# Half of a top-k mask moved off VectorE, ties folded into the comparisons, and a shorter chain for the residual weight

## The chip, the cores and the metric

One of the eight cores of a Trainium2 chip runs the program, once. The metric is the device time of one execution in microseconds. The engines are PE (TensorE: matmuls), DVE (VectorE), ACT (ScalarE), POOL (GpSimd) and SP, which only issues DMAs here. Each takes its own instructions strictly in order, and they wait for one another through semaphores.

## The reference

A layer normalisation, then an attention with 16 heads of 8 columns over 16 batches of 256 tokens, and beside it a product-key feed-forward whose 128 experts are selected per token and head:

```python
xn = _layernorm(x)                                   # x: 16 x 256 x 128
x + attention(xn) + ffn(xn)

# attention, per batch: softmax(q k^T / sqrt(8)) v for 16 heads, then @ Wo
# ffn, per token and each of 8 heads:
ts0, ti0 = top_k(s0, 4); ts1, ti1 = top_k(s1, 4)     # of 32 scores each
comb_s = ts0[..., :, None] + ts1[..., None, :]       # 16 sums
top_s, pos = top_k(comb_s, 16)                       # all 16 of them
w = softmax(top_s)
eh = gelu(down[idx] . xn)
out = sum over the 16 of up[idx] * eh * w
```

The index is `ti0 * 32 + ti1`, and a table has 128 rows, so indices beyond it are clamped to the last expert. The kernel therefore gives every expert (first key 0 to 3, second key 0 to 31) the product of two softmax weights, where both keys are among their best four, and the last expert also gets all the weight that is left.

## The kernel before

After a projection stage (until about 53 us) the program runs `NSLOT` = 128 slots, eight to a batch. A slot is a pair of heads of the attention: PE makes the scores of slot n into `SI` (L676), DVE takes their maxima (L1070), and eleven slots later (`LAG`) PE makes the scores once more into `SJ` with the maxima subtracted (L717), ACT takes the exponential (L475) and PE multiplies with the values (L737). There is one buffer `SJ`, so L717 waits for the exponential of the slot before, and the exponential waits for L717.

The feed-forward filter of one batch is cut into pieces that hang on the slot's number modulo 8, `k`, on each engine, in an order written out by hand. I call eight slots a period. In a period, for the batch before:

- POOL splits the maxima of a whole batch into two bf16 parts (`mpart`, L1320 and L1322, `split_maxima`), PE transposes them (L748), ACT copies them (`mT`, L498), and DMAs bring them to the attention operand. Only then may PE make the filter scores (L759, `scores`, k = 1) into the two banks `psH`.
- ACT copies both banks to `s_sb` (L394, k = 2), DVE finds the best eight of each of 32 rows of 32 (`MAX8`, L1096, k = 2 and 3, 16 heads-and-tiles times two key sets).
- DVE overwrites the best four of the second key set with `NEG` (`MATCH_REPLACE8`, L1109, k = 4 to 7, 16 of them, `REPLACED` cuts them over the slots), and turns that into weights: where `r_sb` equals `NEG` the exponential `z_sb`, else 0 (L1130, one `SCALAR_TENSOR_TENSOR` over 128x512, k = 0).
- POOL scales the scores (L1342 to L1345), subtracts to compare the first four keys with the best four (`order`, L1349) and with each other for ties (L1351 to L1353). ACT takes the sign (L487), squares the ties' part (L490) and turns it into "is equal" (L509). POOL adds the comparisons to a rank (L1366, L1368), adds the ties in three steps (L1374), and selects the keys of rank below 4 (L1376).
- POOL then makes the weights of the first key set (`p0`, L1383), their share (`a0`, L1393) and what is left for the last expert (L1385 to L1396), and the outer products `prod` of both token tiles (L1405, t = 0 at k = 0, t = 1 at k = 1; `FH` = 8 heads each). PE transposes these (L766, k = 3 and 4), and ACT copies them (L451).
- The attention's own output goes PE L779 (k = 5), ACT L482, DVE `rden` (L1124, k = 5, after six of the replacements), POOL `on` (L1311), PE L786, ACT `onT` (L458), PE L794 (k = 7).

Behind the slots stands a tail: the last eleven exponentials (`weights(n)`, L517, with three buffers instead of one), and the whole filter of the last batch `LB` on DVE (L1155 to L1238), while POOL finishes batch `LB - 1`. Its PE order is written out at L876 to L919.

## Time and profile before

| | |
|---|---|
| median of 3 runs | 331.07 us (329.2 to 331.9) |
| the profiled execution | 330.68 us, its span 328.9 us |
| DVE busy | 311.7 us, 95% of the span |
| PE, ACT, POOL busy | 299.7 (91%), 279.3 (85%), 265.7 (81%) us |
| mean of a period in the stage of the slots | 15.6 us |
| granted TensorE clock | 0.995 of full speed |

The span runs from the first to the last instruction; 1.8 us of the execution lie around it. In the stage of the slots all four engines are over 85% busy in every period, so the page alone doesn't say which of them sets the time; the waits within one period do.

### The profile page before, as it was taken

To read this page: it belongs to the slowest core of one execution; us is meant where nothing else is said; L and a number is where in the kernel's file an instruction comes from. 1 tells how busy PE (TensorE), PEld (TensorE's weight loads), DVE (VectorE), ACT (ScalarE), POOL (GpSimd) and SP (SyncE) were. 2 spreads that over 40 slices of the span, in tenths; PEclk is the share of its full clock that TensorE was granted. 3 is DMA by queue.
4 is the path that set the end of the run, shared out by engine and by line. 5 is a ranking of instruction groups with operands and counts; after the bars stand their busy time and mean duration, and the time that the engine had idled before them with its cause. 6 is when DMAs were issued, how large, how long until landed. Compare 5 with 4: busy or idle time off the path is not lost.

```text
span 328.9 us, 9946 instructions
## 1 busy us (share of the span) xinstructions
PE 299.7 (91%) x3181; PEld 165.7 (50%) x3181; DVE 311.7 (95%) x1387; ACT 279.3 (85%) x508; POOL 265.7 (81%) x537
## 2 busy tenths in 40 slices
PE   7999999978898999999999988988989899998796
PEld 3555554343445555555454545554555555555445
DVE  7699999889999999999999999999999999999874
ACT  3799986988888989898889888989888898989681
POOL 7389886835868898989898989898989899898940
PEclk9999999999999999999999999999999999999899
DMA  4866665417221222213130404030403120000001
GB/s 127 219 160 182 181 179 156 122 49 130 52 65 36 65 60 59 76 42 89 29 100 18 117 3 114 4 116 8 110 26 91 38 81 19 4 20 0 21 19 32
DMA packets 45889, 24.83 MB, mean 76 GB/s; under 512 B 5453, under 2 KB 45709, under 8 KB 45837
## 3 DMA queue, kind: packets, MB, share of 16 engines
q1 hardware_dynamic: 45836, 24.20, 27.4%
q8 instruction: 25, 0.41, 0.5%
q14 instruction: 28, 0.22, 0.2%
HBM read 15.54 MB, written 8.39 MB: 73 GB/s over the span
## 4 chain that ended last, share of the span: by engine, by line
DVE 66%; PE 13%; issue 13%; ACT 5%; POOL 2%; POOLq 0%; ACTq 0%
DVE negm L1070 28%; DVE top L1096 13%; DVE r_sb L1109 12%; DVE r_sb L1130 2%; PE SI L590 2%; ACT Eb L418 1%; PE SJ L843 1%; PE SJ L579 1%; ACT Eb L517 1%; DVE st L965 1%; DVE rden L1124 1%; PE SJ L582 1%; DVE Eb L953 1%; DVE fst L988 1%; DVE vhat L929 1%
## 5 line engine op out<-in xcount | busy, mean ns | idle before, releaser
L1070 DVE TENSOR_REDUCE negm<-SI 128x4 f32<-128x1024 f32 x128 | 151.8, 1197 | 1.2 <-PE SI L676 1.2
L475 ACT ACTIVATE Eb<-SJ 128x1024 f32<-128x1024 f32 x117 | 119.7, 1023 | 8.9 <-PE SJ L717 8.8
L737 PE MATMUL bank<-Eb,vhat 128*18 128x256 f32 x1024 | 68.4, 385 | 10.5 <-ACT s_sb L394 10.0
L1405 POOL TENSOR_TENSOR prod<-r_sb,a 128x1024 f32<-128x1024 f32 x28 | 53.5, 1912 | 0.0
L717 PE MATMUL SJ<-QS,KS 50*128 50x256 bf16 x484 | 47.4, 273 | 5.2 <-ACT Eb L475 4.5
L676 PE MATMUL SI<-KS,QS 48*128 48x256 bf16 x512 | 50.1, 271 | 1.1 <-DVE negm L1070 0.8
L1096 DVE MAX8 top<-s_sb 128x8 f32<-128x32 f32 x480 | 47.2, 172 | 0.9 <-ACT s_sb L394 0.9
L737 PEld LDWEIGHTS bank<-Eb,vhat 128*18 128x18 f32 x1024 | 24.2, 97 | 37.7 <-ACT s_sb L394 14.0
L1109 DVE MATCH_REPLACE8 r_sb<-top,s_sb 128x36 f32<-128x36 f32 x240 | 40.2, 176 | 0.0
L676 PEld LDWEIGHTS SI<-KS,QS 48*128 48x128 bf16 x512 | 20.3, 94 | 29.6 <-issue 22.6
L766 PE MATMUL bank<-cst,prod 128*128 128x128 f32 x240 | 33.5, 284 | 0.9 <-POOL prod L1431 0.9
L766 PEld LDWEIGHTS bank<-cst,prod 128*128 128x128 f32 x240 | 26.3, 143 | 7.3 <-issue 7.3
L717 PEld LDWEIGHTS SJ<-QS,KS 50*128 50x128 bf16 x484 | 14.3, 94 | 27.6 <-ACT Eb L475 14.0
L1268 POOL TENSOR_TENSOR Eb<-Eb,parts 128x512 f32<-128x512 f32 x16 | 18.2, 1158 | 10.9 <-ACT parts L332 8.2
L394 ACT ACTIVATE s_sb<-bank 128x512 f32<-128x512 f32 x30 | 16.4, 593 | 4.1 <-PE bank L759 4.1
L759 PE MATMUL bank<-kblk,fqT 64*128 64x128 f32 x240 | 18.5, 284 | 0.5 <-ACT s_sb L394 0.5
L1109 DVE MATCH_VALUE_LOAD r_sb<-top,s_sb 128x8 f32 x240 | 18.4, 77 | 0.0
L759 PEld LDWEIGHTS bank<-kblk,fqT 64*128 64x128 f32 x240 | 15.5, 187 | 3.6 <-ACT mT L498 2.6
L1374 POOL TENSOR_TENSOR rank<-rank,order 128x48 f32<-128x48 f32 (+2 forms) x45 | 12.7, 281 | 4.7 <-ACT order L509 0.5
L1345 POOL TENSOR_TENSOR z_sb<-s_sb,rn 128x512 f32<-128x512 f32 x15 | 15.8, 1053 | 0.0
L794 PE MATMUL bank<-wo_sb,onT 128*128 128x128 f32 x60 | 13.0, 299 | 2.5 <-ACT onT L458 0.8
L1311 POOL TENSOR_TENSOR on<-fwq_in,rden 128x256 f32<-128x256 f32 x14 | 8.8, 629 | 7.1 <-DVE rden L1124 7.1
(223 smaller groups left out, 625.5 us busy)
## 6 DMA issues: line engine op xcount, KB each, us to landing
qk_parts<-parts SPq DMA_DIRECT2D x48, 128.0 KB, 2.4
QS<-qk_parts SPq DMA_DIRECT2D x32, 96.0 KB
KS<-qk_parts SPq DMA_DIRECT2D x32, 96.0 KB
x_sb<-L_attn_x SPq DMA_DIRECT2D x8, 256.0 KB, 3.4
QS<-qk_parts SPq DMA_DIRECT2D x32, 64.0 KB
KS<-qk_parts SPq DMA_DIRECT2D x32, 64.0 KB
out<-ysb SPq DMA_DIRECT2D x16, 128.0 KB, 2.0
QS<-qk_parts SPq DMA_DIRECT2D x32, 32.0 KB
```

Source lines behind the costliest of these rows:

```text
L394: A(half(to[:, :, :, 0:NK], e).rearrange("p q u a k -> p q (u a) k"), src.rearrange("p (q g k) -> p q g k", g=4, k=NK), ACT.Copy).then_inc ...
L475: A(Eb[:, n % 4, :], SJ[:, :], ACT.Exp).then_inc(s["ex"], 1)
L676: last = mm(SI[n % 2][:, (e * BT + t) * S:(e * BT + t + 1) * S], QS[r, b % RING, pr, t * P:(t + 1) * P], KS[r, b % RING, pr, :], start=Tru ...
L717: last = mm(second(n)[:, (e * BT + t) * S:(e * BT + t + 1) * S], KS[r, b % RING, pr, t * P:(t + 1) * P], QS[r, b % RING, pr, :], start=Tru ...
L737: last = mm(psO[32 * c:32 * c + 2 * VC, (q % 2) * S:(q % 2 + 1) * S], vhat[:, v0:v0 + 2 * VC], Eb[:, (2 * g + c // 2) % 4, e0:e0 + S], sta ...
L759: last = mm(dst[e][:, q * P:(q + 1) * P], fqT[rows, r, tok:tok + P], kblk[rows, 4 * e:4 * (e + 1), :].rearrange("p g k -> p (g k)"), start ...
L766: last = mm(dst[:, t * P:(t + 1) * P], prod[:, t, h, :, :].rearrange("p i j -> p (i j)"), ident, start=(h == 0), stop=(h == FH - 1), is_tr ...
L1070: V.tensor_reduce(negm[:, bb % 2, :, :, pr].rearrange("p t e -> p e t"), SI[slot % 2][:, :].rearrange("p (e t j) -> p e t j", e=2, j=S), a ...
L1096: last = V.max(top8[:, h, a, :], s_sb[:, h, a, 0:NK])
L1109: last = V.match_replace(r_sb[:, h, :], top4[:, h, :], s_sb[:, h, 1, :], NEG)
L1268: TT(r32[:, t, :], q32[:, t, :], parts[:, c % 2, t, 0, :], ALU.subtract).then_inc(s["r_" + nm], 1)
L1405: TT(prod[:, t, :, :, :], r_sb[:, hs, 0:NK].unsqueeze(2).to_broadcast([P, FH, TOP, NK]), a0[:, hs, :].unsqueeze(3).to_broadcast([P, FH, TO ...
```

## The change

The mask: `REPLACING` puts the heads of the second token tile first in the row of replacements. DVE's L1130 now covers only the first tile (128x256). For the second tile ACT turns `r_sb` into 1 where it is `NEG` (now -2^126, so that scaled by -2^-125 and less 1 it is exactly 1) and 0 elsewhere, by a Relu at k = 6 in the place of L509, and POOL multiplies it with `z_sb` at k = 1, between the two outer products. The rows of `s_sb` and `r_sb` lose their 4 columns of padding, with which two memsets go (L1252 and L1417, the second in slot 68; the first is replaced by one of `order`).

The ties: `order` keeps them in 4 more columns beside the comparisons. Sign and Square cover 448 and 192 elements (352 and 96 before), and POOL subtracts all at once (a new 128x256 instruction, `df`) in the place of L509 and of the three additions.

The rest: the share `a0` is made first, and the weight that is left is 1 minus its sum times the second denominator, one POOL instruction less.

Besides: `rden` moves three replacements up on DVE; `psH` is turned round, so that PE's `values` at k = 2 waits for the first of the two copies only; in the tail two score groups and one `values` go ahead of `turn_products(0)`, and DVE's maxima of the last batch no longer wait for `sel`.

```diff
-                if k == 6 and 0 <= b < B:
-                    act.wait_ge(s["eq2"], b + 1)
-                    A(ties, ties, ACT.Identity, bias=one, scale=-1.0).then_inc(s["eq"], 1)
+                if k == 6 and 0 <= b < LB - 1:
+                    act.wait_ge(s["mr"], 4 * b + 2)
+                    A(r_sb[:, FH:NH, :], r_sb[:, FH:NH, :], ACT.Relu, bias=less, scale=-2.0 ** -125).then_inc(s["msk"], 1)
...
-                    A(order[:, :, :], order[:, :, :], ACT.Sign).then_inc(s["sg"], 1)
+                    A(compared, compared, ACT.Sign).then_inc(s["sg"], 1)
...
-                    V.scalar_tensor_tensor(r_sb[:, :, 0:NK], r_sb[:, :, 0:NK], NEG, z_sb[:, :, 0:NK],
+                    V.scalar_tensor_tensor(r_sb[:, 0:FH, :], r_sb[:, 0:FH, :], NEG, z_sb[:, 0:FH, 0:NK],
                                            ALU.is_equal, ALU.mult).then_inc(s["es"], 1)
...
-                    pool.wait_ge(s["sg"], b + 1)
+                    pool.wait_ge(s["eq2"], b + 1)
+                    TT(cmp[:, :, :, :], cmp[:, :, :, :], ties[:, :, :, :], ALU.subtract).then_inc(s["df"], 1)
+                    pool.wait_ge(s["df"], b + 1)
...
+                    if t == 1:
+                        pool.wait_ge(s["msk"], b + 1)
+                        pool.wait_ge(s["z1e"], b + 1)
+                        TT(r_sb[:, FH:NH, :], r_sb[:, FH:NH, :], z_sb[:, FH:NH, 0:NK], ALU.mult).then_inc(s["em"], 1)
+                        pool.wait_ge(s["em"], b + 1)
...
-        psH = [psM, psO]
+        psH = [psO, psM]
...
-                    pe.wait_ge(s["fs_ev"], 2 * (slot // 8))
+                    pe.wait_ge(s["fs_ev"], 2 * (slot // 8) - 1)
                     values(m // 2)
...
             sj(N0 + 3)
+            sj(N0 + 4)
+            values(4 * LB - 1)
+            sj(N0 + 5)
             pe.wait_ge(s["mt_ev"], B)
             pe.wait_ge(s["pr"], 4 * LB - 2)
             turn_products(0, psM)
-            sj(N0 + 4)
-            values(4 * LB - 1)
-            sj(N0 + 5)
...
-                if slot == 68:
-
-                    pool.wait_ge(s["fs"], 10)
-                    V.memset(s_last[:, :, :, NK:KP], NEG).then_inc(s["pad2"], 1)
```

POOL's queue in a period, from `on` of one batch to the first outer product, before:

```order
L1311 TENSOR_TENSOR on<-fwq_in,rden 128x256 [waits s_onp,s_ct_ev,s_rd]
L1366 TENSOR_TENSOR cm<-order 128x128 [waits s_sg]
L1374 TENSOR_TENSOR rank<-rank,order 128x16x3 [waits s_rk,s_eq]
L1374 TENSOR_TENSOR rank<-rank,order 128x16x2 [waits s_rk]
L1374 TENSOR_TENSOR rank<-rank,order 128x16 [waits s_rk]
L1322 TENSOR_TENSOR mpart<-negm,mpart 128x4x8 [waits s_mh]
L1383 TENSOR_TENSOR p<-rank,z_sb 128x64 [waits s_sel,s_ze]
L1389 TENSOR_TENSOR dinv<-dd,den 128x16 [waits s_fe]
L1405 TENSOR_TENSOR prod<-r_sb,a 128x1024 [waits s_wt,s_es,s_fa]
```

and now (here up to the second outer product; rows that are as before are left out in both):

```order
L1368 TENSOR_TENSOR order<-order 128x64x4 [waits s_eq2]
L1370 TENSOR_TENSOR cm<-order 128x128 [waits s_df]
L1322 TENSOR_TENSOR mpart<-negm,mpart 128x4x8 [waits s_mh]
L1383 TENSOR_TENSOR p<-rank,z_sb 128x64 [waits s_sel,s_ze]
L1386 TENSOR_TENSOR a<-p,dd 128x64 [waits s_fe,s_p0]
L1395 TENSOR_SCALAR p0r<-p0r 128x16 [waits s_p2]
L1409 TENSOR_TENSOR prod<-r_sb,a 128x1024 [waits s_wt,s_es,s_fa]
L1402 TENSOR_TENSOR r_sb<-r_sb,z_sb 128x256 [waits s_z1e,s_msk]
L1409 TENSOR_TENSOR prod<-r_sb,a 128x1024 [waits s_es,s_wt,s_fa,s_em]
```

Ahead of `mpart` three small instructions have become one of 128x256, and behind it another of 128x256 has come between the outer products.

PE's queue in the tail, from `sj(N0 + 3)` (into `SJ`) on, before:

```order
L717 MATMUL SJ<-QS,KS 128x256 [waits s_ex,s_mrow]
L717 MATMUL SJ<-QS,KS 128x256 x3
L766 MATMUL bank<-cst,prod 128x128 [waits s_pr,s_mt_ev]
L766 MATMUL bank<-cst,prod 128x128 x7
L717 MATMUL SI<-QS,KS 128x256 [waits s_ex]
L717 MATMUL SI<-QS,KS 128x256 x3
L737 MATMUL bank<-Eb,vhat 18x256 [waits s_ex]
L737 MATMUL bank<-Eb,vhat 18x256 x7
```

and now:

```order
L718 MATMUL SJ<-QS,KS 128x256 [waits s_ex,s_mrow]
L718 MATMUL SJ<-QS,KS 128x256 x3
L718 MATMUL SI<-QS,KS 128x256 [waits s_ex]
L718 MATMUL SI<-QS,KS 128x256 x3
L738 MATMUL bank<-Eb,vhat 18x256 [waits s_ex]
L738 MATMUL bank<-Eb,vhat 18x256 x7
L718 MATMUL SI<-QS,KS 128x256 [waits s_ex]
L718 MATMUL SI<-QS,KS 128x256 x3
L767 MATMUL bank<-cst,prod 128x128 [waits s_pr,s_mt_ev]
```

The transposes, which wait for POOL's products (`s_pr`), now stand behind two groups of scores that feed ACT.

## Rows read from the trace of the kernel before

**Rows 1.** Windows of one period each: length, then busy time of each engine
```profile
177.84:193.41 15.57, 14.38 (x177) 8.10 (x176) 15.57 (x77) 13.82 (x26) 13.98 (x32) 1.00 0.23 63
193.41:209.55 16.14, 14.31 (x177) 8.09 (x176) 15.65 (x77) 13.68 (x26) 14.23 (x33) 1.00 0.21 59
```

**Rows 2.** Lines of DVE: busy us, mean ns of one, idle before
```profile
L1109 DVE MATCH_REPLACE8 r_sb<-top,s_sb 128x36 f32<-128x36 f32 x240 | 40.2, 176 | 0.0
L1130 DVE SCALAR_TENSOR_TENSOR r_sb<-r_sb,z_sb 128x512 f32<-128x512 f32 x14 | 9.5, 676 | 0.0
...
L1222 DVE SCALAR_TENSOR_TENSOR fqT<-fqT,z_sb 128x256 f32<-128x256 f32 x2 | 0.8, 430 | 0.0
```

**Rows 3.** Timeline of POOL: start, duration in us
```profile
211.18 0.77 POOL L1383 TENSOR_TENSOR p<-rank,z_sb 128x64 f32<-128x64 f32 x1
...
221.16 0.73 POOL L1298 TENSOR_TENSOR wgT<-wgT,xnT 128x256 f32<-128x256 f32 x1
222.39 0.63 POOL L1311 TENSOR_TENSOR on<-fwq_in,rden 128x256 f32<-128x256 f32 x1 [0.50 <-DVE rden L1124]
...
224.76 0.98 POOL L1374 TENSOR_TENSOR rank<-rank,order 128x48 f32<-128x48 f32 x3
```

**Rows 4.** Lines of POOL
```profile
L1374 POOL TENSOR_TENSOR rank<-rank,order 128x32 f32<-128x32 f32 x15 | 4.5, 301 | 1.2
...
L1389 POOL TENSOR_TENSOR dinv<-dd,den 128x16 f32<-128x16 f32 x15 | 3.3, 222 | 0.0
```

**Rows 5.** Timeline of POOL around slot 68
```profile
194.52 0.20 POOL L1417 MEMSET fqT<- 128x128 f32 x1
...
194.97 0.75 POOL L1322 TENSOR_TENSOR mpart<-negm,mpart 128x32 bf16<-128x32 f32 x1
```

**Rows 6.** Timeline of DVE around slot 68
```profile
194.95 0.67 DVE L1130 SCALAR_TENSOR_TENSOR r_sb<-r_sb,z_sb 128x512 f32<-128x512 f32 x1
...
198.37 0.75 DVE L1096 MAX8 top<-s_sb 128x8 f32<-128x32 f32 x7 [0.48 <-ACT s_sb L394]
```

**Rows 7.** Timeline of PE over one period and a little more
```profile
221.13 0.39 PE L717 MATMUL SJ<-QS,KS 50*128 50x256 bf16 x4 [0.25 <-ACT Eb L475]
...
226.85 0.29 PE L748 MATMUL bank<-cst,mpart 128*32 128x128 bf16 x2
...
229.95 1.06 PE L737 MATMUL bank<-Eb,vhat 128*18 128x256 f32 x16 [0.74 <-ACT s_sb L394]
230.96 0.39 PE L717 MATMUL SJ<-QS,KS 50*128 50x256 bf16 x4
```

**Rows 8.** Timeline of ACT in the same period
```profile
220.05 1.02 ACT L475 ACTIVATE Eb<-SJ 128x1024 f32<-128x1024 f32 x1
...
221.26 0.50 ACT L487 ACTIVATE order<-order 128x352 f32<-128x352 f32 x1
221.65 1.02 ACT L475 ACTIVATE Eb<-SJ 128x1024 f32<-128x1024 f32 x1
...
229.78 1.03 ACT L475 ACTIVATE Eb<-SJ 128x1024 f32<-128x1024 f32 x1
```

**Rows 9.** Lines of ACT
```profile
L487 ACT ACTIVATE order<-order 128x352 f32<-128x352 f32 x15 | 7.5, 501 | 0.9 <-POOL order L1353 0.9
...
L490 ACT ACTIVATE order<-order 128x96 f32<-128x96 f32 x15 | 4.4, 290 | 0.0
```

**Rows 10.** Timeline of PE in the tail
```profile
309.24 1.87 PE L766 MATMUL bank<-cst,prod 128*128 128x128 f32 x8 [0.91 <-POOL prod L1431]
```

**Rows 11.** Timeline of ACT in the tail
```profile
311.69 1.02 ACT L517 ACTIVATE Eb<-SI 128x1024 f32<-128x1024 f32 x1 [2.29 <-PE SI L717]
```

**Rows 12.** Timeline of DVE in the tail
```profile
305.14 3.08 DVE L1163 MAX8 top<-fqT 128x8 f32<-128x32 f32 x32 [0.99 <-POOL rank L1376]
...
314.86 0.42 DVE L1135 TENSOR_TENSOR wgT<-bank,xnT 128x256 f32<-128x256 f32 x1 [1.45 <-PE bank L766]
...
318.18 0.36 DVE L1141 RECIPROCAL rden<-bank 128x32 f32<-128x32 f32 x1 [0.65 <-PE bank L779]
```

More of the change, by code:

```diff
@@ L28 @@
 P = 128
-NEG = -1.0e20
+NEG = -2.0 ** 126
 C_ID, C_AVG, C_GRP = 0, 128, 256
@@ L65, in program @@
     TOP = 4
-    KP = NK + TOP
     E = down.shape[0]
@@ L116, in program @@
         nm = ve
-        eps = sb("eps", [P, 2]); one = eps[:, 1:2]
+        eps = sb("eps", [P, 2]); less = eps[:, 1:2]
         vhat = sb("vhat", [P, VC + NT * VT])
@@ L182, in program @@
         HEADS = [4 * q + 2 * e + u for e in range(2) for q in range(NH // 4) for u in range(2)]
+        REPLACING = [h for h in HEADS if h >= FH] + [h for h in HEADS if h < FH]
         def half(a, e):
@@ L486, in _ @@
                     act.wait_ge(s["tie"], b + 1)
-                    A(order[:, :, :], order[:, :, :], ACT.Sign).then_inc(s["sg"], 1)
+                    A(compared, compared, ACT.Sign).then_inc(s["sg"], 1)
                 if k == 6 and 0 <= b < B:
                     act.wait_ge(s["sg"], b + 1)
-                    A(ties, ties, ACT.Square).then_inc(s["eq2"], 1)
+                    A(tied, tied, ACT.Square).then_inc(s["eq2"], 1)
                 if k == 0 and m >= -1:
@@ L926, in _ @@
             V.memset(onT[:, 0:P // 2], 0.0).then_inc(s["zeros"], 1)
-            V.memset(one, 1.0)
+            V.memset(less, -1.0)
             V.memset(eps[:, 0:1], LN_EPS).then_inc(s["eps"], 1)
@@ L1059, in inverse_squares, with inverse_heads @@
                 V.reciprocal(rn_t[:, i * P:(i + 1) * P], rn_t[:, i * P:(i + 1) * P]).then_inc(s["n2r"], 1)
+            def inverse_heads(b):
+                dve.wait_ge(s["ct_ev"], b + 1)
+                if b >= 1:
+                    dve.wait_ge(s["on"], b)
+                V.reciprocal(rden[:, :].rearrange("p (c u) -> p c u", u=2), heads[:, :, :, DH]).then_inc(s["rd"], 1)
             for slot in range(NSLOT):
@@ L1105, in _ @@
                     for i in range(REPLACED[quarter], REPLACED[quarter + 1]):
-                        if quarter == 1 and i == FH:
-                            dve.wait_ge(s["t4"], 2 * b + 2)
-                        h = HEADS[i]
+                        if quarter == 1 and i == FH - 1 and b >= 1:
+                            inverse_heads(b - 1)
+                        h = REPLACING[i]
                         last = V.match_replace(r_sb[:, h, :], top4[:, h, :], s_sb[:, h, 1, :], NEG)
@@ L1117, in _ @@
                     V.reciprocal(dd[:, :], both).then_inc(s["fe"], 1)
-                b = (slot - LAG - 10) // 8
-                if k == 5 and 0 <= b < B:
-                    dve.wait_ge(s["ct_ev"], b + 1)
-                    if b >= 1:
-                        dve.wait_ge(s["on"], b)
-                    V.reciprocal(rden[:, :].rearrange("p (c u) -> p c u", u=2), heads[:, :, :, DH]).then_inc(s["rd"], 1)
                 b = slot // 8 - 2
@@ L1156, in _ @@
                                    ALU.is_equal, ALU.mult).then_inc(s["es"], 1)
-            dve.wait_ge(s["sel"], LB)
+            dve.wait_ge(s["tie"], LB)
             dve.wait_ge(s["t4"], 2 * LB)
@@ L1175, in _ @@
             dve.wait_ge(s["p0"], LB)
+            dve.wait_ge(s["sel"], LB)
             dve.wait_ge(s["t8"], 2 * B)
@@ L1211, in _ @@
             V.reciprocal(dd[:, :], both).then_inc(s["fe"], 1)
-            dve.wait_ge(s["tie"], LB + 2)
-            for i, (lo, n, at) in enumerate(((1, 3, 0), (2, 2, 3), (3, 1, 5))):
-                dve.wait_ge(s["rk"], 4 * LB + i + 1)
-                V.tensor_tensor(rank[:, 0, :, lo:TOP], rank[:, 0, :, lo:TOP], ties[:, :, at:at + n], ALU.add).then_inc(s["rk"], 1)
-            dve.wait_ge(s["rk"], 4 * LB + 4)
+            dve.wait_ge(s["rk"], B)
             V.tensor_scalar(rank[:, 1, :, :], rank[:, 0, :, :], float(TOP), None, ALU.is_lt).then_inc(s["sel"], 1)
@@ L1251, in _ @@
             V.memset(v_tiles(0, VSPLIT)[:, :, DH:VC], 1.0).then_inc(s["vone"], 1)
-            V.memset(s_sb[:, :, :, NK:KP], NEG)
+            V.memset(order[:, :, :, :], 1.0)
             V.memset(top4[:, :, TOP:8], NEG).then_inc(s["pad"], 1)
@@ L1370, in _ @@
                         split_maxima(LB)
-                    pool.wait_ge(s["eq"], b + 1)
-                    for i, (lo, n, at) in enumerate(((1, 3, 0), (2, 2, 3), (3, 1, 5))):
-                        pool.wait_ge(s["rk"], 4 * b + i + 1)
-                        TT(rank[:, 0, :, lo:TOP], rank[:, 0, :, lo:TOP], ties[:, :, at:at + n], ALU.add).then_inc(s["rk"], 1)
-                    pool.wait_ge(s["rk"], 4 * b + 4)
-                    V.tensor_scalar(rank[:, 1, :, :], rank[:, 0, :, :], float(TOP), None, ALU.is_lt).then_inc(s["sel"], 1)
+                    pool.wait_ge(s["rk"], b + 1)
+                    V.tensor_scalar(rank[:, 1, :, :], rank[:, 0, :, :], 0.0, None, ALU.is_lt).then_inc(s["sel"], 1)
                 if k == 7 and slot // 8 < LB:
```

55 lines of the change are left out of this document (29 added, 26 removed), and 2 rows, old and new, of the table names.

## The prediction

> **What bounds the kernel now.** I read three views. The windows, cut at one period each, come first: DVE is busy for all 15.57 us of a normal period, and one period took 16.14 [rows 1]. A queue with no idle time sets the pace. But PE has 14.38 us in the same window and POOL 13.98 [rows 1], so a gain on DVE is only worth what the second slowest allows. The second view, the timelines of the other engines, is for that question: a queue that doesn't wait for DVE anywhere has the same length as DVE's by itself.
>
> *POOL* waits once in a period for DVE: 0.50 us ahead of `on`, for `rden` [rows 3]. The rest of its idle time is the gap between links of its own chains, 1.2 us over 15, so 0.08 each [rows 4]. Its own length is 15.57 - 0.50 = 15.07 us.
>
> *PE and ACT* pass the one buffer `SJ` to and fro, and the third view is their timelines in the same period. PE waits 0.25 us for an exponential and 0.74 us for ACT's copy of the filter scores [rows 7]: both are waits inside the pair. The place where the pair could wait for POOL is L748, and there the wait before its first matmul is at most some 0.04 us: I see no row with a wait on POOL or on DVE. So the pair has a cycle of its own of about 15.5 us. Three loops of 15.57, 15.07 and some 15.53 us turn side by side.
>
> **The change part by part, one period.** *DVE.* L1130 shrinks from 512 to 256 columns: 676 ns before; L1222 is the same operation at 256 and takes 430 [rows 2]: -0.246. The replacements read 32 instead of 36 columns; the nearest rate is that of the two rows just used, 246 ns for 256 columns, 0.96 ns each, so 16 x 4 x 0.96 = -0.06. DVE's loop: 15.57 - 0.31 = 15.26 us. `rden` costs the same, three replacements earlier.
>
> *POOL.* Out: the three additions, 0.98 us and a gap [rows 3, 4], -1.06; and the wait for `rden`, which comes three replacements earlier, by 0.5 us, about what the wait was. Within the rest chain one instruction of 0.22 us goes [rows 4], but the five that stay behind `p0` now each wait for the one before, where some pairs ran gapless: with 0.08 for each new gap and 0.12 of overlap that is lost I take +0.15. In: two instructions of 128x256, `df` and the mask's product. Their price isn't in the trace; the nearest rows are 0.63 and 0.73 us for the same number of elements [rows 3], and each has a link behind it, 0.08: 1.42 to 1.62, I take 1.56, nearer to 0.73, since neither reads a broadcast operand and L1298 doesn't either. The sum: 15.07 - 1.06 + 0.15 + 1.56 = 15.72.
>
> From this comes off what L1130 does to POOL. L1383 took 0.77 us [rows 3], and in the disturbed period it was L1322, of 32 elements, that took 0.75 [rows 5], each time right behind the start of L1130, which at 194.95 lasts until 195.62 [rows 6]. A POOL instruction that meets L1130 stands still until it has ended. The shorter L1130 holds it up 0.25 us less. POOL's loop: 15.47 us; bounds 15.33 (both new ones at 0.63) and 15.7 (nothing comes off).
>
> The rule behind this is in the Trainium skill, SBUF — State Buffer, section "Who interferes with whom": a DVE instruction with two SBUF inputs and a GpSimd instruction that reads SBUF exclude each other for a whole instruction, whichever began first. The rows show only the one direction, GpSimd held up; the other is a rival below.
>
> *PE and ACT.* ACT's Sign grows from 352 to 448 elements, Square from 96 to 192; with 501 and 290 ns [rows 9] an element costs 211 / 256 = 0.82 ns, so +0.08 each. Relu over 256 comes out as 290 + 160 x 0.82 = 421 ns by the same rows (bounds 0.42 and 0.55, a bias operand) in the place of L509. Square and Relu lie ahead of `onT`, for which ACT waits anyway, and cost nothing there; without that cover they would cost 0.1 to 0.2. Sign isn't covered: the exponential at 221.65 starts when Sign lets it, 1.60 after the one at 220.05 [rows 8], so +0.08 is on the pair's path. Against this, `values` at k = 2 waits for one copy instead of two. Its 0.74 us shrink by about the half, but the next scores then wait for the exponential: that ends at 229.78 + 1.03 = 230.81, handing over takes 0.06 (220.05 + 1.02 against 221.13), so 230.87 instead of 230.96 [rows 7, 8]: -0.09. With `on` and `mpart` ready earlier some 0.03 at each of L786 and L748: -0.06. The pair: 15.57 - 0.07 = 15.50 us. Bounds: 15.65 (nothing gained, Sign and Relu both on the path) and 15.35 (the whole 0.3 of the copy comes through).
>
> So DVE wins 0.31 us and the period 0.07, as PE and ACT become the bound with POOL 0.03 behind. There are 14 such periods (L1130 x14 [rows 2]): **-1.0 us**.
>
> *The period with the memset.* Slot 68's memset, 0.20 us [rows 5], pushed L1322 into the start of L1130 (194.97 behind 194.95 [rows 5, 6]), `mpart` came 0.5 us late, and through L748, `mT`, L759 and the copy DVE stood for 0.48 [rows 6]; the period lost 0.57 [rows 1]. The memset goes: **-0.57 us**, bounds 0 (L1322 meets L1130 another time) and 0.57.
>
> *The tail.* PE waits 0.91 us for POOL's product and then takes 1.87 us for eight transposes [rows 10], with the scores for ACT queued behind; ACT stands 2.29 us [rows 11]. Now two groups of scores go ahead, and ACT runs on. But the last outputs hang on DVE too, so what counts is DVE's chain of the last batch. Its waits: 0.99 for `sel`, 1.45 for PE L766, 0.65 for PE L779 [rows 12]. The first is replaced by the wait for `s_last`, copied only around the same moment: I take 0.1 from it. The second goes whole if POOL's products are made as early as before: the transposes then follow each other on PE at about 311.0 and 312.4, before DVE comes by at 313.4 (314.86 - 1.45). Of the third I take half, 0.3, and 0.1 from narrower replacements. **-2.0 us**, bounds -0.2 (another wait of DVE takes over) and -2.9.
>
> Sum against the profiled execution's 330.68 us: 330.68 - 1.0 - 0.57 - 2.0 = 327.1. This execution lies 0.4 below the median of 331.07, well inside the three runs' spread; I keep 327.1.
>
> **The rivals.** (1) *DVE's gain comes through whole.* If the pair's waits are the shadow of DVE's pace and not a loop of their own, the period falls to POOL's lower bound or DVE's 15.26. For it: DVE is the only one without idle time. Against: no row of PE or ACT shows slack towards the others, and POOL sums to 15.47. 14 x 0.31 = 4.3: 330.68 - 4.3 - 0.57 - 2.0 = 323.8.
>
> (2) *The tail gives nothing back.* DVE's chain from 305.14 on has its waits, but each can be followed by the next: ACT's exponential of `z_sb`, POOL's `p0` and `a0`. 330.68 - 1.0 - 0.57 - 0.2 = 328.9.
>
> (3) *POOL becomes the bound.* Both new instructions at their upper price and nothing off for the shorter L1130: 15.7, so +0.13 x 14 = +1.8: 330.68 + 1.8 - 0.57 - 2.0 = 329.9.
>
> (4) *Slower: L1322 meets L1130 in every period.* POOL's work ahead of `mpart` and behind it changes by more than half a microsecond each, so its phase against DVE moves. If L1322 starts within L1130, `mpart` is late and DVE stands as in rows 6, and the next period starts from the same phase. The price of one is 0.57 [rows 1], with L1130 shorter by 0.25 about 0.3 to 0.57, and 14 of these from the period before: +4.2 to +8, with the tail's gain 330.68 + 8 - 2 = 336.7 at the worst, 333 to 337. It decides once POOL's own period exceeds some 15.6, so that L1322 falls back behind the start of L1130. For it: it did happen, from 0.2 us of added work. Against: POOL gains 0.5 us by `rden` and L1322 now has less ahead of it.
>
> The skill's rule named above adds a thing to this rival: DVE too would stand, behind a GpSimd instruction that has begun. Where L1130 meets POOL's chain of 0.2 to 0.3 us instructions, that would cost DVE up to 0.3 us in a period, and DVE has about as much to spare now; no row here shows it in the stage of the slots.
>
> **How the numbers follow.** My forecast has 0.47 (325.8 to 328.4 as its own range), (1) 0.17, (2) 0.18, (3) 0.10, (4) 0.08. The time is that of the likeliest, 327.1. The range from 323.6 to 330.2 takes in (1), (2) and (3) and leaves out (4) and the ends. About 1% can be told from no change here, that is 3.3 us of 331.07: below 327.8 lie (1) and about three quarters of the forecast, together 0.52; above 334.4 most of (4), 0.07; the rest, 0.41, is the same.
>
> **What would show it.** In the profile of after: L1130 at about 430 ns; DVE with idle time in a period, 0.2 us, ahead of the maxima of SI or of the first MAX8; a period of 15.50 and none of 16.1; POOL's two new instructions between 0.63 and 0.73, and its wait for `rden` gone; PE's wait for the copy near 0.3; the Sign near 0.58; in the tail no wait of ACT above 1 us, and DVE's 1.45 gone. Wrong would be: a period of 15.3 with DVE full (rival 1), L1322 at 0.5 or more in many periods (rival 4), POOL without any wait and a period above 15.6 (rival 3), or DVE's waits in the tail that add up to 3 us as before (rival 2).

## The result, and the profile after

| | before | after |
|---|---|---|
| median | 331.5 us (329.2 to 334.3, 13 runs) | 328.85 us (327.4 to 331.2, 13 runs) |
| ratio, 95% interval | | 0.9934 (0.9908 to 0.9961) |
| profiled execution, span | 330.68, 328.9 us | 328.70, 326.9 us |
| DVE, PE, ACT, POOL busy | 311.7, 299.7, 279.3, 265.7 us | 309.0, 298.9, 280.4, 265.5 us |

The change saves 0.7%, 2.2 us (1.3 to 3.0), where 4.0 were forecast; a second measurement of the changed kernel (e11) gave 0.9921 (0.9892 to 0.9949), 2.6 us. I cut both profiled executions at the first and the last start of L1130, of which there are 14 in each, with 13 periods between them:

| us | before | after | difference |
|---|---|---|---|
| start to the first L1130 | 85.97 | 87.33 | +1.36 |
| from there to the last L1130 (13 periods) | 202.98 | 202.06 | -0.92 |
| from the last L1130 to the end | 39.95 | 37.52 | -2.43 |

The middle row is the steady work. Before, it was twelve periods of 15.57 and one of 16.13; now it is 15.23, 15.44 and eleven of 15.58. So nearly all of it comes from the one long period (-0.56) and from the first two (-0.46); the normal period, from which 1.0 us was to come, has not become shorter at all. These are the windows of two such periods, with the columns of [rows 1]:

```profile
195.96:211.54 15.58, 14.37 (x178) 8.08 (x180) 15.46 (x77) 13.90 (x26) 14.14 (x31) 1.00 0.23 61
211.54:227.12 15.58, 14.37 (x178) 8.08 (x180) 15.46 (x77) 13.90 (x26) 14.13 (x31) 1.00 0.22 63
```

DVE, the third busy time, is no longer busy throughout: it stands some 0.2 us ahead of its first MAX8 (L1104), where 0.2 was forecast, and 0.05 ahead of `rden`. The chain of the work that ended last, which before was 66% DVE, now names PE and ACT:

```profile
PE 59%; ACT 19%; DVE 12%; issue 6%; POOL 4%; POOLq 0%; ACTq 0%; DVEq 0%
```

The other views of after answer to the groups ahead of the prediction. DVE's lines, for [rows 2]:

```profile
L1116 DVE MATCH_REPLACE8 r_sb<-top,s_sb 128x32 f32<-128x32 f32 x240 | 39.7, 177 | 0.0
L1130 DVE SCALAR_TENSOR_TENSOR r_sb<-r_sb,z_sb 128x256 f32<-128x256 f32 x14 | 6.8, 484 | 0.0
```

The lines of POOL and ACT that are new or larger, for [rows 4] and [rows 9]: `df`, the mask's product, Sign, Square and Relu.

```profile
L1368 POOL TENSOR_TENSOR order<-order 128x256 f32<-128x256 f32 x15 | 10.9, 727 | 1.0 <-ACT order L492 1.0
L1402 POOL TENSOR_TENSOR r_sb<-r_sb,z_sb 128x256 f32<-128x256 f32 x14 | 10.3, 733 | 0.0
...
L489 ACT ACTIVATE order<-order 128x448 f32<-128x448 f32 x15 | 8.7, 582 | 0.7 <-POOL order L1355 0.7
L492 ACT ACTIVATE order<-order 128x192 f32<-128x192 f32 x15 | 5.5, 370 | 0.0
L511 ACT ACTIVATE r_sb<-r_sb,eps 128x256 f32<-128x256 f32 x14 | 7.2, 514 | 0.0
```

The timeline of POOL in the period from 211.5, for [rows 3]: start, duration, and in brackets the idle time before and its releaser. The wait for `rden` at `on` (L1311) is small now and no longer named; the one that is named is 0.20 us for DVE's maxima.

```profile
211.46 0.24 POOL L1389 TENSOR_TENSOR p0s<-a 128x32 f32<-128x32 f32 x1
211.77 0.28 POOL L1391 TENSOR_TENSOR p0r<-p0s 128x16 f32<-128x16 f32 x1
...
218.65 0.30 POOL L1344 TENSOR_TENSOR z_sb<-s_sb,rn 128x64 f32<-128x64 f32 x1 [0.20 <-DVE top L1104]
...
221.50 0.72 POOL L1298 TENSOR_TENSOR wgT<-wgT,xnT 128x256 f32<-128x256 f32 x1
222.34 0.63 POOL L1311 TENSOR_TENSOR on<-fwq_in,rden 128x256 f32<-128x256 f32 x1
```

But it isn't gone altogether. DVE's `rden` ends at 222.26, and `on` starts 0.08 behind it:

```profile
221.91 0.35 DVE L1067 RECIPROCAL rden<-fwq_in 128x32 f32<-128x32 f32 x1
```

L1298 ends at 222.22, and where `on` has nothing to wait for it starts 0.04 before the recorded end of the one before (as in every second period of e10). So 0.16 us of waiting are left here and 0.24 at L1344 (its 0.20 and the same 0.04), and POOL's own length is 15.58 - 0.40, about 15.2 us.

The timelines of PE and of ACT in the same period, for [rows 7] and [rows 8]:

```profile
214.38 1.06 PE L738 MATMUL bank<-Eb,vhat 128*18 128x256 f32 x16 [0.26 <-ACT s_sb L396]
215.88 0.40 PE L718 MATMUL SJ<-QS,KS 50*128 50x256 bf16 x4 [0.44 <-ACT Eb L477]
```

```profile
214.71 1.03 ACT L477 ACTIVATE Eb<-SJ 128x1024 f32<-128x1024 f32 x1
...
220.55 1.02 ACT L477 ACTIVATE Eb<-SJ 128x1024 f32<-128x1024 f32 x1
221.47 0.41 ACT L484 ACTIVATE fwq_in<-bank 128x288 f32<-128x288 f32 x1
221.76 0.58 ACT L489 ACTIVATE order<-order 128x448 f32<-128x448 f32 x1
222.22 1.02 ACT L477 ACTIVATE Eb<-SJ 128x1024 f32<-128x1024 f32 x1
```

Two things are to be seen. PE's wait for the copy shrank from 0.74 to 0.26 us, but the next scores now wait 0.44 us for the exponential: and the scores start 1.17 us behind the exponential's start (214.71 to 215.88), as before (1.18, from 229.78 to 230.96 in [rows 7, 8]). Nothing was won there, where 0.09 was counted on. And the two exponentials around the Sign start 1.67 us apart (220.55 to 222.22), 1.60 before [rows 8]: the Sign's growth lies on the path in full.

The tail, for [rows 12]. DVE's waits were 0.99, 1.45 and 0.65 us; now the second is gone:

```profile
305.71 3.07 DVE L1163 MAX8 top<-fqT 128x8 f32<-128x32 f32 x32 [1.08 <-ACT fqT L396]
...
313.26 0.42 DVE L1135 TENSOR_TENSOR wgT<-bank,xnT 128x256 f32<-128x256 f32 x1
...
316.15 0.36 DVE L1141 RECIPROCAL rden<-bank 128x32 f32<-128x32 f32 x1 [0.21 <-PE bank L780]
```

Last, the granted TensorE clock, which the prediction had left out. First two windows in the tail of the kernel before, with the busy times of PE, PE's weight loads, DVE, ACT and POOL, then the granted clock:

```profile
305.00:310.00 5.00, 3.28 (x40) 1.56 (x33) 4.56 (x50) 4.08 (x9) 4.62 (x11) 0.93 0.11 31
310.00:315.00 5.00, 5.00 (x46) 2.63 (x44) 3.55 (x23) 2.47 (x4) 3.19 (x3) 0.73 0.09 26
```

And two windows in the projection stage of the kernel after, where the kernel before has 1.00 in both:

```profile
5.00:10.00 5.00, 3.80 (x18) 2.46 (x18) 2.54 (x19) 2.95 (x10) 1.83 (x4) 0.80 0.60 159
10.00:15.00 5.00, 5.00 (x14) 2.22 (x13) 3.22 (x9) 2.94 (x8) 0.79 (x1) 0.86 0.99 268
```

Part of the time the clock stood at its lower level, 1.2 GHz. In the tail before, it fell right behind PE's wait of 0.91 us, and the eight transposes that followed took 1.87 us [rows 10] instead of the 1.09 that a second group of eight takes in the same tail. In the kernel after, the fall comes near the start (between 7.5 and 12 us), and the whole delay of 1.43 us arises there: the first maxima of the slots begin at 54.5 instead of 53.05 us, and that is the +1.36 of the first table. So the two profiled executions each hold a stretch of low clock, at different places.

### The profile page after: what moved, and what is told of

The parts are those of the page before. It is cut to its first block, busy times and chain, and to the rows that moved or that the text cites. A ratio compares the mean times of both kernels' runs of the same rounds, so it can differ in the third digit from the quotient of the medians.

```text
span 326.9 us, 9939 instructions
## 1 busy us (share of the span) xinstructions
PE 298.9 (91%) x3181; PEld 165.6 (51%) x3181; DVE 309.0 (95%) x1385; ACT 280.4 (86%) x507; POOL 265.5 (81%) x505
## 4 chain that ended last, share of the span: by engine, by line
PE 59%; ACT 19%; DVE 12%; issue 6%; POOL 4%; POOLq 0%; ACTq 0%; DVEq 0%
PE bank L738 12%; PE SJ L718 10%; ACT Eb L477 9%; PE bank L767 8%; PE SI L677 6%; PE bank L760 4%; PE bank L795 3%; ACT s_sb L396 3%; ACT onT L460 2%; PE bank L796 2%; PE bank L787 2%; PE SI L591 2%; ACT Eb L420 1%; ACT Eb L519 1%; PE SJ L844 1%
## 5 line engine op out<-in xcount | busy, mean ns | idle before, releaser
L1104 DVE MAX8 top<-s_sb 128x8 f32<-128x32 f32 x480 | 47.5, 177 | 1.9 <-ACT s_sb L396 0.5
L1116 DVE MATCH_REPLACE8 r_sb<-top,s_sb 128x32 f32<-128x32 f32 x240 | 39.7, 177 | 0.0
L767 PE MATMUL bank<-cst,prod 128*128 128x128 f32 x240 | 32.8, 280 | 0.0
L718 PEld LDWEIGHTS SJ<-QS,KS 50*128 50x128 bf16 x484 | 14.3, 94 | 35.6 <-ACT Eb L477 15.2
L1116 DVE MATCH_VALUE_LOAD r_sb<-top,s_sb 128x8 f32 x240 | 19.2, 80 | 0.0
L760 PEld LDWEIGHTS bank<-kblk,fqT 64*128 64x128 f32 x240 | 15.5, 187 | 3.6 <-ACT mT L500 2.6
L1344 POOL TENSOR_TENSOR z_sb<-s_sb,rn 128x64 f32<-128x64 f32 x15 | 4.6, 305 | 12.3 <-DVE top L1104 12.3
L358 ACT ACTIVATE Eb<-x_sb,ve,rs 128x128 f32<-128x128 f32 x32 | 13.1, 479 | 1.7 <-DVE ve L979 1.7
```

What stands on the lines that cost most here:

```text
L718: last = mm(second(n)[:, (e * BT + t) * S:(e * BT + t + 1) * S], KS[r, b % RING, pr, t * P:(t + 1) * P], QS[r, b % RING, pr, :], start=Tru ...
L760: last = mm(dst[e][:, q * P:(q + 1) * P], fqT[rows, r, tok:tok + P], kblk[rows, 4 * e:4 * (e + 1), :].rearrange("p g k -> p (g k)"), start ...
L767: last = mm(dst[:, t * P:(t + 1) * P], prod[:, t, h, :, :].rearrange("p i j -> p (i j)"), ident, start=(h == 0), stop=(h == FH - 1), is_tr ...
L1104: last = V.max(top8[:, h, a, :], s_sb[:, h, a, 0:NK])
L1116: last = V.match_replace(r_sb[:, h, :], top4[:, h, :], s_sb[:, h, 1, :], NEG)
```

## The experiments

Each is a kernel of its own, compared with the kernel before on the same chip.

**Is it PE and ACT that hold the period now?** e1 changes nothing but the place of ACT's second copy of the filter scores, from before the exponential of slot k = 2 to behind it:

```diff
-                    for e in range(2):
-                        filter_scores(s_sb, e, psH[e])
+                    filter_scores(s_sb, 0, psH[0])
...
                     A(Eb[:, n % 4, :], SJ[:, :], ACT.Exp).then_inc(s["ex"], 1)
+                if k == 2 and 1 <= b < B:
+                    filter_scores(s_sb, 1, psH[1])
```

> The changed kernel with one edit on ACT: at k = 2 the second of the two copies of the filter scores (L396) stands behind the exponential instead of ahead of it. ACT, PE, DVE and POOL do the same work. Theory A (the loop of PE and ACT over the one buffer SJ is what holds the period at 15.58 us in the changed kernel, DVE and POOL have 0.20 us to spare): the exponential at k = 2 starts 0.48 us earlier, the period falls to the next bound, some 15.38 us, 14 x 0.2 = 2.8 us less in all. Theory B (DVE's queue, 15.46 us busy, or a loop through all engines holds it): nothing or below 0.5 us. Theory C (the scores at k = 3 wait for the DMA of mT, which the table of waits names 15 times): these scores stay 3.41 us behind the end of the copy of mT, and the period stays 15.58.

Measured: 325.96 us (324.9 to 326.8, 4 runs), ratio 0.9854 (0.9823 to 0.9884); the period is 15.38 to 15.40, and the tail 37.20. No engine has less to do; one wait moved. PE's timeline shows that the wait of 0.44 us for the exponential is gone:

```profile
212.03 1.06 PE L739 MATMUL bank<-Eb,vhat 128*18 128x256 f32 x16 [0.26 <-ACT s_sb L396]
213.03 0.40 PE L719 MATMUL SJ<-QS,KS 50*128 50x256 bf16 x4
```

So the pair held the changed kernel's period at 15.58. Theory C falls as well: these scores now start 2.92 us behind the end of the copy of `mT` (209.74 + 0.37 in ACT's timeline), not 3.41.

**Did it need DVE's part of the change?** e8 gives the kernel before this same rearrangement of PE and ACT, and leaves DVE's 512 columns:

```diff
-        psH = [psM, psO]
+        psH = [psO, psM]
...
-                    pe.wait_ge(s["fs_ev"], 2 * (slot // 8))
+                    pe.wait_ge(s["fs_ev"], 2 * (slot // 8) - 1)
...
                    A(Eb[:, n % 4, :], SJ[:, :], ACT.Exp).then_inc(s["ex"], 1)
+                if k == 2 and 1 <= b < B:
+                    filter_scores(s_sb, 1, psH[1])
```

> The kernel before with PE's and ACT's part of e1 alone: psH turned round, values waits for one copy, and the second copy of the filter scores goes behind the exponential. DVE's L1130 still covers 512 columns. Theory A (three loops side by side: the pair's falls from 15.50 to some 15.31, but DVE's own 15.57 stays): period 15.57 as before, 330.9 to 331.4 us, ratio 1.000 (0.998 to 1.001). Theory B (the pair's loop is what e1 shortened and DVE only shadows it): 14 periods of -0.18, 328.7 us, ratio 0.992.

Measured: 331.3 us (10 runs), ratio 1.0019 (0.9986 to 1.0053); twelve periods between 15.56 and 15.59 and one of 16.13. Theory A: without the relief of DVE it is worth nothing. And e2 gives the kernel before the relief of DVE alone (the mask of the second token tile is left out, nothing takes its place):

```diff
-                    V.scalar_tensor_tensor(r_sb[:, :, 0:NK], r_sb[:, :, 0:NK], NEG, z_sb[:, :, 0:NK],
+                    V.scalar_tensor_tensor(r_sb[:, 0:FH, 0:NK], r_sb[:, 0:FH, 0:NK], NEG, z_sb[:, 0:FH, 0:NK],
```

> The kernel before with L1130 over 128x256 instead of 128x512, and nothing in its place (the mask of the second token tile is left out, so the output is not the reference's). Theory A: PE and ACT had a loop of 15.57 us of their own already, so DVE's 0.25 us come to nothing: period 15.55 to 15.57, DVE gets 0.2 us idle, time as before within 0.3% (the period with slot 68's memset may lose its 0.57 us). Theory B: DVE held the period: 15.32, that is 14 x 0.25 = 3.5 us less, 1.1%.

Measured: 329.57 us (10 runs), ratio 0.9947 (0.9919 to 0.9975). The period is 15.50 us, between the two theories and much nearer to A (the first one is 15.30, the one with the memset 15.88). DVE and POOL both wait in it (DVE 0.1 to 0.2 us for the copy of the filter scores, POOL 0.59 for `rden`), so what is left is the pair: 15.50 is its own length in the kernel before, 0.07 below DVE's, and all that a relief of DVE alone could bring in a normal period. From the first to the last L1130 e2 takes 201.67 us, less than the changed kernel's 202.06: there the relief is the same, and the Sign's growth stands against it. In a window of the length of [rows 1] DVE is no longer busy throughout, and PE's and ACT's work is as it was; POOL's 13.98 us are 13.76, since it stands less behind the shorter L1130:

```profile
177.84:193.41 15.57, 14.36 (x184) 8.16 (x180) 15.46 (x77) 13.78 (x26) 13.76 (x32) 1.00 0.24 62
```

(The window is cut 0.07 longer than the period.)

**What does the longer Sign cost?** e5 is the changed kernel, e6 is e1, each with a Sign over 64 of the 448 elements, so that most of the signs are left out:

```diff
-                    A(compared, compared, ACT.Sign).then_inc(s["sg"], 1)
+                    A(compared[:, :, 0:1], compared[:, :, 0:1], ACT.Sign).then_inc(s["sg"], 1)
```

> The changed kernel with ACT's Sign cut from 448 to 64 elements, so most signs of the comparisons are left out; nothing else is touched. Theory A (PE and ACT set the changed kernel's period of 15.58 us, and the longer Sign stands on their path: the interval between the exponentials around it rose from 1.60 to 1.67 us): that interval falls to some 1.50, the period to 15.42 (DVE and POOL, whose own lengths are 15.38, then bind), 13 periods of -0.16 make -2.1 us: 326.6 to 326.9, ratio to the kernel before 0.986 to 0.988. Theory B (the pair only follows DVE or POOL, or the DMA of mT): the period stays 15.58 and the time 328.9, ratio 0.993.

Measured: 326.73 us (4 runs), ratio 0.9899 (0.9847 to 0.9952), period 15.43 to 15.44, the exponentials around the Sign 1.51 apart (221.67 to 223.18 below). Theory A, to 0.02 us a period. Its profiled execution (328.97) starts its first maxima at 56.1 us, as e8 does (last section), and has a stretch of low clock behind the projection stage; the other three runs lie at 326.6 to 326.8.

```profile
221.67 1.02 ACT L477 ACTIVATE Eb<-SJ 128x1024 f32<-128x1024 f32 x1
222.59 0.41 ACT L484 ACTIVATE fwq_in<-bank 128x288 f32<-128x288 f32 x1
222.88 0.32 ACT L489 ACTIVATE order<-order 128x64 f32<-128x64 f32 x1
223.18 1.02 ACT L477 ACTIVATE Eb<-SJ 128x1024 f32<-128x1024 f32 x1
```

> As e1_after_split (the second copy of the filter scores behind the exponential), with ACT's Sign cut to 64 elements as in e5. Theory A (in e1 the pair was no longer the bound and DVE and POOL, 15.38 each by themselves, set its period of 15.39): nothing more is gained, period 15.38 to 15.40, 325.9 to 326.2 us, ratio 0.985. Theory B (the pair was still the bound in e1): the period falls by the Sign's share to about 15.25, 14 x 0.14 = 2.0 us less: 324.0 us, ratio 0.979.

Measured: 324.14 us (323.6 to 325.5, 4 runs), ratio 0.9811 (0.9766 to 0.9857), period 15.30 to 15.33. This lies between the two theories, and both had a number wrong. In this trace DVE waits nowhere in a period, so 15.32 is its own length and the bound. The 15.38 that I had read for it still held a wait: in e1 DVE stands 0.06 us ahead of its first MAX8. POOL still waits 0.14 us for DVE here (0.09 at `on`, 0.05 at L1345), so its own length is about 15.2, as in the changed kernel. The Sign still cost 0.08 in e1: there ACT waits 0.20 us for POOL's tie differences ahead of it, and then it stands in front of an exponential.

**Where does the tail's gain come from?** e3 gives the kernel before the new order of PE's tail alone:

```diff
             sj(N0 + 3)
+            sj(N0 + 4)
+            values(4 * LB - 1)
+            sj(N0 + 5)
             pe.wait_ge(s["mt_ev"], B)
             pe.wait_ge(s["pr"], 4 * LB - 2)
             turn_products(0, psM)
-            sj(N0 + 4)
-            values(4 * LB - 1)
-            sj(N0 + 5)
```

> The kernel before with PE's order in the tail of the changed one alone: two score groups and one values ahead of the transposes of POOL's products. If this order is the tail's gain: from the last L1130 to the end 37.6 us instead of 39.95 (37.51 in the changed kernel), 2.3 us in all, 0.7%. If the gain came from DVE no longer waiting for sel or from POOL's earlier products: below 0.5 us.

Measured: 330.28 us (10 runs), ratio 0.9969 (0.9951 to 0.9987), tail 38.31 us. e7 is the counterpart, the changed kernel with the same lines turned back:

```diff
+            pe.wait_ge(s["mt_ev"], B)
+            pe.wait_ge(s["pr"], 4 * LB - 2)
+            turn_products(0, psM)
             sj(N0 + 4)
             values(4 * LB - 1)
             sj(N0 + 5)
-            pe.wait_ge(s["mt_ev"], B)
-            pe.wait_ge(s["pr"], 4 * LB - 2)
-            turn_products(0, psM)
```

> The changed kernel with PE's old order in the tail: the transposes of the first outer products stand again ahead of two groups of scores. Theory A (the tail got shorter through this order, as the prediction had it: ACT's 2.29 us and DVE's 1.45 us of waiting went with it): both waits come back, the tail from the last L1130 on grows from 37.5 to about 39 us, 330.3 to 330.8 us, ratio 0.998. Theory B (the order is worth little at the full clock, as e3 and e4 have it, 38.33 and 38.39; the tail's real gain of 0.9 us is that of POOL's earlier products and the shorter DVE chain): the tail is at most 37.8 us where the granted clock stays at 1.0, the time 328.9 to 329.3, ratio 0.993 to 0.995. If the granted clock falls in the tail again, PE stands some 0.8 us or more for POOL's product just ahead of it, and the tail is up to 1.5 us longer.

Measured: 329.44 us (328.3 to 331.2, 10 runs), ratio 0.9973 (0.9946 to 1.0001), tail 37.57 us against 37.52. Theory B: in the changed kernel the order is worth 0.05 us, and its old form shows why. PE comes to the transposes, and the product is there; it doesn't wait:

```profile
308.79 1.09 PE L767 MATMUL bank<-cst,prod 128*128 128x128 f32 x8
```

**The memset of slot 68.** e4 is the kernel before with that memset two slots earlier, out of the way of L1322:

```diff
-                if slot == 68:
+                if slot == 66:
```

> The kernel before with POOL's memset of s_last issued in slot 66 instead of slot 68, behind the outer products instead of ahead of the split of the maxima. Expected if the memset pushed L1322 into the start of L1130: no period of 16.14 us, all 15.57, 0.57 us less in the profile (too little for the times). If the long period had another cause: it stays, there or elsewhere.

Measured: 329.91 us (6 runs), ratio 0.9988 (0.9952 to 1.0024). All periods are 15.57, the one of 16.13 is gone. This trace has also the kernel before with a clock of 1.00 in the whole tail, and this tail is 38.39 us, not 39.95. PE waits as in [rows 10], but the transposes take 1.06 us and not 1.87:

```profile
308.72 1.06 PE L766 MATMUL bank<-cst,prod 128*128 128x128 f32 x8 [0.89 <-POOL prod L1431]
```

In ACT's and DVE's timelines of that tail the waits of 2.29 and 1.45 us are 1.25 and 0.45. So 1.56 us of the kernel before's tail was the low clock, not the wait. The tail's gain at the full clock is 38.39 - 37.52 = 0.87 us, and by e7 PE's order has at most 0.05 of it. What has changed is POOL: its first product of the tail ends 20.16 us behind the last L1130 in e4 and 19.16 in after.

**How much of that is `rden`?** e9 is the changed kernel with DVE's reciprocal back behind three more replacements:

```diff
-                        if quarter == 1 and i == FH - 1 and b >= 1:
-                            inverse_heads(b - 1)
...
                     last.then_inc(s["mr"], 1)
+                    if quarter == 1 and b >= 1:
+                        inverse_heads(b - 1)
```

> The changed kernel with DVE's reciprocal rden moved back behind three more replacements, where it stood before. Theory A (the earlier rden is what makes POOL fast enough for the rest of the change, in the slots and in the tail, where POOL's products come 1.0 us earlier after the last L1130 than in e4): POOL waits about 0.45 us for rden again, has only 0.20 us to spare in a period, and the period grows from 15.58 to some 15.8; the tail from 37.5 to about 38.0; together +3 to +3.8 us, 332 us, ratio 1.00 to 1.005. Theory B (the wait stands beside the pair's own loop and costs nothing there, as in the kernel before): period 15.58, only the tail grows by 0.5, 329.4 us, ratio 0.995.

Measured: 330.26 us (10 runs), ratio 0.9971 (0.9944 to 0.9998), tail 37.84, and periods that alternate, after one of 15.89, between 15.58 and 15.72 (from first to last L1130 203.04 us against 202.06). Neither theory: the wait of POOL is back, 0.35 us in one period and 0.23 in the next, and costs 0.07 us a period, 1.0 in all, and 0.3 in the tail.

```profile
223.54 0.63 POOL L1311 TENSOR_TENSOR on<-fwq_in,rden 128x256 f32<-128x256 f32 x1 [0.35 <-DVE rden L1067]
```

So one reciprocal three replacements earlier, which costs nothing, carries 1.3 us of the result: without it the slots would be no faster than before. How it carries them isn't separated: in e9 POOL also meets L1130 with another instruction (L1386, 0.47 us instead of 0.30).

**Is e1 the better kernel?** e10 is e1 again, e11 the changed kernel itself, on one chip.

> The kernel of e1 once more, in more rounds and beside the changed kernel on the same chip (e11). If e1's gain is real: period 15.39 to 15.40, 325.5 to 326.3 us, 0.8 to 0.9% below the changed kernel, ratio to the kernel before 0.982 to 0.987. If it was owed to the clock of its profiled run: within 0.3% of the changed kernel.

> The changed kernel itself, unaltered, for the direct comparison with e10 and for a second trace of it: 328.6 to 329.1 us, ratio 0.992 to 0.995, period 15.58. If the granted clock stays at 1.0 in its prologue and its tail, the first maxima start at 53.0 instead of 54.5 us and the time is 327.2 to 327.5; its tail, which has no wait of PE for POOL's product, stays at 37.5.

Measured: e10 327.62 us (326.0 to 328.1, 6 runs), ratio 0.9873 (0.9837 to 0.9909); e11 328.92 us (327.4 to 329.8, 8 runs), ratio 0.9921. e11 came as expected. e10 missed both of its theories: its period is not 15.39, and its time is 0.4% under that of e11, half of what e1 had shown. e1's kernel is the better one both times, by 0.8% (0.9854 against 0.9934) and by 0.5% (0.9873 against 0.9921, on one chip, where the two intervals overlap); in the traces its 13 periods are 2.1 and 1.1 us shorter.

The difference between e1 and e10 can be read: the periods of e10 alternate between 15.42 and 15.51, since POOL meets L1131 otherwise. Here POOL and DVE in e10:

```profile
211.29 0.41 DVE L1131 SCALAR_TENSOR_TENSOR r_sb<-r_sb,z_sb 128x256 f32<-128x256 f32 x1
```

```profile
211.31 0.49 POOL L1390 TENSOR_TENSOR p0s<-a 128x32 f32<-128x32 f32 x1
```

POOL's instruction of 32 elements takes 0.49 us, or up to 0.53, in all these periods, where it takes 0.24 in e1, and L1131 takes 0.41 instead of 0.49. POOL has no wait left in every second of these periods, so this is its own loop: about 15.2 and the stall, together 15.42, above DVE's 15.32.

The changed kernel does the same in e11, and there it costs nothing. POOL's and DVE's rows of e11:

```profile
211.70 0.52 POOL L1389 TENSOR_TENSOR p0s<-a 128x32 f32<-128x32 f32 x1
```

```profile
211.72 0.41 DVE L1130 SCALAR_TENSOR_TENSOR r_sb<-r_sb,z_sb 128x256 f32<-128x256 f32 x1
```

POOL's wait of 0.20 us at L1344 has become its stall here, and the period is 15.58 as in after, since the pair sets it. So one kernel runs in two ways, with its starts shifted by some 0.02 us: POOL's instruction begins 0.03 us before L1130 in every normal period of after, e1 and e7, and DVE stands; it begins between 0.02 before and 0.01 behind it in e10 and e11, and POOL stands. What puts an execution into one or the other is not shown. It isn't the low clock from 75 to 80 us alone: e10 has it and e11 has not, and e6 has it and runs like e1. In e11 the clock is low from 7 to 11 us (0.73 and 0.93 in the two windows shown for after), its first maxima start at 54.7 us, and its period and tail are those of after, 15.58 and 37.53.

## Why the prediction was wrong, and where it was right

**The period (-0.07 x 14 = -1.0): the step that failed.** The bound was named rightly: DVE was relieved and PE and ACT set the pace; DVE idles, and rival 1 fell. The terms that failed are the two gains that were set against the Sign's +0.08, -0.09 for the copy and -0.06 at L786 and L748: neither came. The pair's own length before is 15.50 (e2), the Sign adds 0.08 as worked out (1.60 to 1.67), and 15.50 + 0.08 is the 15.58 that was measured, with nothing left for a gain. The Relu took 0.51 us and not 0.42, which leaves no mark in this sum. The slack of 0.07 under DVE is what the Sign ate. A second error hid half of the first: the pair's own cycle was read as "about 15.5" and "some 15.53", and then the terms were added to DVE's 15.57. From 15.50 they would have given 15.43. So the forecast of 15.50 is nearer to the measured 15.58 than its reasoning was, by luck. The sum also took 14 such periods; there are 13, and one of them is the memset's. Why the copy was worth nothing: the prediction counted a handover of 0.06 us from the exponential to the scores, as at the other slots, but at this place the scores start 1.17 us after the exponential's start, in both kernels, 0.14 behind its end. With 0.14 for the handover the exponential would not have let them start before 230.95 in the kernel before either, and they started at 230.96. What I gave to `on` (-0.03 at L786) is there only in the sense of e9: it prevents a loss of 0.07.

**The first two periods (-0.46).** No step had them: 15.23 and 15.44. In e2 the first is shorter too, 15.30. The likely reason is that POOL and ACT don't have a whole batch's work yet; no run tests it. They make up for nearly half of the 1.0 us that the normal periods didn't bring.

**The memset (-0.57): right,** -0.56 in the change, and e4 has it alone (16.13 to 15.57), with the mechanism of [rows 5, 6].

**The tail (-2.0): the size came out in the profile, for a wrong reason.** The profiled executions differ by 2.43 us, of which 1.56 are the clock in [rows 10 to 12]. The prediction took the durations of a stretch of lower clock (1.87 us for eight transposes) for durations of the kernel, and the 1.45 and 2.29 us of waiting that followed from them for waits that an order removes. At full clock 0.45 of DVE's 1.45 us is left, and this goes because POOL's products come 1.0 us earlier; 0.44 of the third wait went as well (0.3 was taken), and these two make the 0.87 us. The first wait, from which 0.1 was taken, grew from 0.99 to 1.08. The second was credited to PE's order, with POOL's products as early as before. They came earlier, and the order had next to no part in it (e7).

But the order isn't worthless in the kernel before: e3 gained 0.3%, about 1.0 us, with a tail that is at full clock only 0.08 us shorter. Its runs show where this may come from: the mean granted clock was at least 0.999 in 5 of 10 runs of e3 and in 4 of the 59 runs of the kernel before that stood beside the three groups of experiments. So without PE's wait the clock seems to have fallen less often, a gain in how often and not in how long, which no sum of durations holds. The changed kernel, which doesn't have the wait either, reached 0.999 in only 3 of 13 runs, so this is not settled.

**POOL (15.47, bounds 15.33 and 15.7).** Both new instructions cost the upper price, 0.73 us and a link of 0.08. Its own length is nevertheless about 15.2, under the lower bound. The largest part is the stall at L1130: in the kernel before L1383 stood 0.45 us (0.77 instead of 0.32), in after L1391 stands 0.06, so 0.39 went and not 0.25. Where POOL stands longer (e11) it is 15.42. Rival 3 fell by this.

**DVE (15.26).** It is 15.32 (e6, where DVE has no idle time). The narrower replacements saved next to nothing (176 to 177 ns each, against 0.96 ns a column that I took from another operation: 0.06 of the sum), and L1130 takes 484 ns and not 430. The latter is the second half of the rule that the prediction weighed: in after, L1130 starts at 211.49 right behind POOL's L1389, which had begun at 211.46, and stands 0.08 us; POOL's L1391 in its turn takes 0.28 us instead of 0.22. That rule is in the Trainium skill, SBUF — State Buffer, section "Who interferes with whom": of two such instructions the one that issues first keeps the other out for its whole length. The traces agree that either can stand for the other: 0.49 us for L1130 where POOL was 0.03 us ahead (after), 0.41 where it was not, and then 0.49 to 0.53 for POOL's 0.24 (e10, e11). Two details they don't bear out. In e11 POOL stands although its start is recorded 0.01 to 0.02 us before L1130's, so recorded starts this close don't tell which issued first. And the stall is shorter than the other's recorded length: L1130 stands 0.08 us, where L1389 is recorded for 0.21 us more.

**Rival 4** (a POOL instruction meets L1130 in every period) came with L1389 in place of L1322, so `mpart` was never late. In after the overlap costs 0.08 us on DVE and 0.06 on POOL; in e11, the same kernel, 0.28 at L1389 in POOL's queue in every period. Neither costs the changed kernel any time, as both queues have more than that to spare below the pair's 15.58. In e10, where the pair is faster, it costs 0.07 us a period on average (200.91 us for 13 periods against e1's 199.96).

**The time.** The steady parts give -0.92 in the loop, -0.87 in the tail and -0.07 in the stretch from the first maxima to the first L1130 (32.92 to 32.85 us): -1.86, within the interval of 1.3 to 3.0. The forecast of 327.1 lay 1.75 us under the median. That the median is in its range owes something to luck: more than half of this gain is the memset and the first two periods, and the normal period, the purpose of the change, gave nothing.

**What stays open.** Why e7 measured 0.4% more than the changed kernel (the intervals overlap) although loop and tail agree to 0.05 us: four of its ten runs lie at a span of 329.2 to 329.4 with a clock of 0.99, and three of the 13 of after at 329.3 to 329.4 with 0.98 to 0.99; none of these was profiled. And why the clock falls near the start in four traces of the changed kernel's family (after, e7, e9, e11) and not in e1, e5, e6 or e10, which have the same code there. In these four PE's first ten matmuls (L617, from 0.97 us on) had taken 3.8 to 4.2 us together, in all others 4.45. And what decides which of POOL and DVE stands at L1130.

## What to carry to other kernels

Where three loops turn side by side, measure the own length of the second before you price a relief of the first: cut the first's work in half in one run (e2), and the period that is left is all that this relief alone can win, before anything new is put on the second's path. Where the pair sets the pace, an instruction that grows between two exponentials is on the path (0.07 to 0.08 us of it in after), while one that moves behind the exponential may give back more than all the rest (e1: -0.19 us a period, for no work; e8: nothing, while DVE still sets the pace). And before durations of a tail are put into a sum, look at the granted clock of that stretch: here 1.56 of 39.95 us were clock.
